# Attention with hand-placed projection steps: projection units of a batch on other steps, norming in place on ScalarE

## What is computed

```python
h = group_norm(x, w, b)                       # 32 groups of 16 channels
q, k, v = split(einsum('oc,bcn->bon', qkv_w, h) + qkv_b)   # 8 heads of 64
attn = softmax(einsum('bhdi,bhdj->bhij', q, k) * 64 ** -0.5)
out = einsum('bhij,bhdj->bhdi', attn, v)
x1 = x + einsum('oc,bcn->bon', proj_w, out) + proj_b
```

## Time and profile before

| what | us |
|---|---|
| median of three runs | 3378.47 |
| the profiled execution | 3384.99 |
| its span, first to last instruction | 3383.0 |
| PE busy | 2937.5 (87%) |
| DVE busy | 2124.9 (63%) |
| ACT busy | 1588.4 (47%) |
| POOL busy | 443.2 (13%) |

### The profile page before, as it was taken

One profiled execution on the slowest core, in us unless ns is written; L12 is line 12 of the kernel. 1 busy time (PEld: TensorE's weight loads), 2 busy tenths in 40 slices (PEclk: granted clock), 3 DMA queues, 4 the chain that ended last, 5 costly groups with the idle time before them and its releaser, 6 DMA issues. The chain is left out here.

```text
span 3383.0 us, 34913 instructions
## 1 busy us (share of the span) xinstructions
PE 2937.5 (87%) x12368; PEld 2375.9 (70%) x12368; DVE 2124.9 (63%) x3224; ACT 1588.4 (47%) x1935; POOL 443.2 (13%) x193
## 2 busy tenths in 40 slices
PE   4998998999899999989998998999755877777877
PEld 2776886788688778868876786888544666656656
DVE  5686767768776776777677677757624435435443
ACT  2565656556564555656456555646521222212221
POOL 1012111100210120021012002011101100111000
PEclk8999999999899999989999999999977988888888
DMA  6222131222123122212312131232030100111100
GB/s 217 60 57 63 54 110 44 63 88 76 57 59 113 48 63 71 84 37 79 113 47 70 53 100 38 82 102 58 19 121 25 50 37 37 37 37 50 43 31 25
DMA packets 131084, 221.52 MB, mean 65 GB/s; under 512 B 50048, under 2 KB 50304, under 8 KB 130432
## 3 DMA queue, kind: packets, MB, share of 16 engines
q1 hardware_dynamic: 130944, 219.69, 21.1%
HBM read 143.34 MB, written 42.21 MB: 55 GB/s over the span
## 5 line engine op out<-in xcount | busy, mean ns | idle before, releaser
L590 DVE TENSOR_REDUCE row_max<-pmax 128x1 f32<-128x512 f32 x1024 | 703.2, 687 | 602.5 <-PE pmax L389 599.0
L484 ACT ACTIVATE p_high<-ring 128x1024 fp32r<-128x1024 f32 x512 | 525.1, 1026 | 730.6 <-PE ring L410 730.4
L606 DVE TENSOR_TENSOR p_low<-p_full,p_high 128x1024 fp32r<-128x1024 f32 x512 | 665.1, 1299 | 6.3 <-ACT p_full L487 6.3
L389 PE MATMUL pmax<-k_high_low,q_high_high 128*128 128x512 f32 x1024 | 459.5, 449 | 98.9 <-DVE row_max L590 96.1
L487 ACT ACTIVATE p_full<-ring 128x1024 f32<-128x1024 f32 x512 | 520.9, 1017 | 0.0
L389 PEld LDWEIGHTS pmax<-k_high_low,q_high_high 128*128 128x128 f32 x1024 | 316.5, 309 | 221.0 <-DVE row_max L590 135.5
L767 POOL TENSOR_TENSOR o_normed<-num_den,o_normed 64x1024 f32<-64x1024 f32 x64 | 173.1, 2705 | 1961.4 <-DMA o_normed<-rec_rows 1943.6
L426 PE MATMUL pv<-p_high,v_high 128*128 128x512 f32 x1024 | 411.9, 402 | 0.0
L427 PE MATMUL pv<-p_high,v_low 128*128 128x512 f32 x1024 | 406.9, 397 | 0.0
L344 PE MATMUL fill<-h_high,w_high 128*128 128x512 f32 x768 | 309.2, 403 | 39.4 <-DVE q_low_max L619 17.1
L410 PE MATMUL ring<-q_low_max,k_high_one 65*128 65x512 f32 x1024 | 330.9, 405 | 1.9 <-DMA q_low_max<-row_max_top 1.9
(11 more groups left out here) (161 smaller groups left out, 3748.6 us busy)
## 6 DMA issues: line engine op xcount, KB each, us to landing
x_tiles<-in_x SPq DMA_DIRECT2D x64, 512.0 KB, 5.4
w_high<-w_split SPq DMA_DIRECT2D x128, 256.0 KB, 2.9
w_low<-w_split SPq DMA_DIRECT2D x128, 256.0 KB, 2.9
k_high_one<-k_high_low SPq DMA_DIRECT2D x128, 128.0 KB, 2.3
q_high_high<-q_high_high SPq DMA_DIRECT2D x128, 128.0 KB, 2.3
o_normed<-rec_rows SPq DMA_DIRECT2D x64, 256.0 KB, 3.5
...
```

What stands on the lines that cost most here:

```text
L389: mm(pmax[:, :], q1[:, q_slot(h), first:first + HALF - 3:4], k1[:, k_slot(h), n * HALF:(n + 1) * HALF], start=True, stop=True).then_inc(s_ ...
L484: nc.scalar.activation(ph[:, r, :], ring[:, r, :], ACT.Exp, scale=ATT_SCALE).then_inc(s_ph, 1)
L590: nc.vector.reduce_max(mcol[:, h % 2, n, i:i + 1], pmax[:, :], AX_X).then_inc(s_mx, 1)
L606: tt(pl[:, r, :], p32[:, r, :], ph[:, r, :].bitcast(F32), ALU.subtract).then_inc(s_pl, 1)
```

## The change

The units of each pair get their steps from a table, and several functions change engine or place.

- **Projection units.** The steps of the units of one batch, before and after (a and b are the two halves of a spread unit, "+" joins units of one step; o is numbered in its order, two for each of four tiles):

| head | before: step: unit | after: step: unit |
|---|---|---|
| 0 | 0,1: k0; 2,3: k1; 4,5: q0; 6,7: none | 0: k0; 1: k1; 2: v0; 3: v1a+vt0; 4: v1b; 5: vt1; 6,7: q0 |
| 1 | 0: q1; 1: v0; 2: v1+vt0; 3: o1; 4: o2+vt1; 5,6,7: o3 to o5 | 0: q1; 1 to 7: o1 to o7 |
| 2 | 0,1,2: o6 to o8; 3,4: k0; 5,6: k1; 7: q0 | 0: o8; 1,2: k0; 3,4: k1; 5,6: q0; 7: none |
| 3 | 0,1: q1; 2,3: v0; 4: v1a; 5: v1b+vt0; 6: none; 7: vt1 | 0,1: q1; 2,3: v0; 4: v1a+vt0; 5: v1b; 6: vt1; 7: none |
| 4 | 0,1: k0; 2,3: k1; 4,5: q0; 6: g0; 7: none | 0,1: k0; 2: g0; 3,4: k1; 5: g1; 6,7: q0 |
| 5 | 0: q1+g1; 1: v0; 2: v1+vt0; 3: none; 4: vt1; 5,6,7: none | 0,1: q1; 2,3: v0; 4: v1a+vt0; 5: v1b; 6: vt1; 7: none |
| 6 | 0,1: none; 2,3: k0; 4,5: k1; 6,7: q0 | the same |
| 7 | 0,1: q1; 2,3: v0; 4: v1a; 5: v1b+vt0; 6: none; 7: vt1 | 0,1: q1; 2,3: v0; 4: v1a+vt0; 5: v1b; 6: vt1; 7: none |

- **Group norm.** The statistics move to steps 3.1, 3.3, 3.4 and 3.5, the scale to 5.0.
- **Norming.** ACT writes the full normed value in place in steps 5.1 to 5.4 (`normed_full`), and reads it again for the high part in 5.5, 5.6, 5.7 and 6.0 (`normed_high`). The norming on DVE is gone. `h_low` stays on POOL, at the same place in its order, and waits for the high part. In the prologue ACT does both for each tile.
- **SP.** The store of the last tile of x1, the load after it and the reload of x each move one step up.

```diff
+PAIR_STEPS = (begins(0, 1, 6, 8, 2, 3, 3, 5, whole=(("k", 0), ("k", 1), ("v", 0), ("q", 1))),
...
-            for s in range(5):
-                put(b, 3 + s, o[s])
-            for s in range(3):
-                put(a + 2, s, o[5 + s])
+            for s in range(7):
+                put(b, 1 + s, o[s])
+            put(a + 2, 0, o[7])
...
-            put(a, 6, ("g", b0 + 1, 0))
-            put(b, 0, ("g", b0 + 1, 1))
+            put(a, 2, ("g", b0 + 1, 0))
+            put(a, 5, ("g", b0 + 1, 1))
...
-            def normed(b, t):
-                if t == 0:
-                    act.wait_ge(s_gab, b + 1)
-                    if b > 0:
-                        act.wait_ge(s_unit, unit(("v", PAIRS * b - 1, 1)))
+            def normed_full(b, t):
+                act.wait_ge(s_gab, b + 1)
                 a, c = gs[:, 6, t:t + 1], gs[:, 7, t:t + 1]
-                nc.scalar.activation(hh[:, t, :], xs[:, t, :], ACT.Identity, bias=c, scale=a).then_inc(s_hh, 1)
+                nc.scalar.activation(xs[:, t, :], xs[:, t, :], ACT.Identity, bias=c, scale=a).then_inc(s_h32, 1)
+            def normed_high(b, t):
+                if b > 0 and t >= 1:
+                    act.wait_ge(s_unit, unit(("v", PAIRS * b - 1, 1)))
+                act.wait_ge(s_h32, bt((b, t)))
+                nc.scalar.activation(hh[:, t, :], xs[:, t, :], ACT.Copy).then_inc(s_hh, 1)
...
-                if h % HEADS == 5 and b < BATCH and 3 <= s <= 6:
-                    normed(b, s - 3)
+                if h % HEADS == 5 and b < BATCH and 1 <= s <= 4:
+                    normed_full(b, s - 1)
+                if h % HEADS == 5 and b < BATCH and s >= 5:
+                    normed_high(b, s - 5)
+                if h % HEADS == 6 and b < BATCH and s == 0:
+                    normed_high(b, CT - 1)
...
-            def normed_full(b, t):
-                dve.wait_ge(s_hh, bt((b, t)))
-                dve.wait_ge(s_gab, b + 1)
-                nc.vector.tensor_scalar(xs[:, t, :], xs[:, t, :], gs[:, 6, t:t + 1], gs[:, 7, t:t + 1],
-                                        ALU.mult, ALU.add).then_inc(s_h32, 1)
...
-                    if h % HEADS == 4 and 1 <= s <= 4:
-                        tile_stats(b, s - 1)
-                    if h % HEADS == 5 and s == 2:
+                    if h % HEADS == 3 and s in (1, 3, 4, 5):
+                        tile_stats(b, (1, 3, 4, 5).index(s))
+                    if h % HEADS == 5 and s == 0:
                         group_scale(b)
-                    if h % HEADS == 5 and 3 <= s <= 6:
-                        normed_full(b, s - 3)
...
+            def rstd(b):
+                pool.wait_ge(s_gst, gst((b, "var")))
+                if b > 0:
+                    pool.wait_ge(s_on, HEADS * (b - 1) + 4)
...
             def h_low(b, t):
-                pool.wait_ge(s_h32, bt((b, t)))
+                pool.wait_ge(s_hh, bt((b, t)))
```

More of the change, by code:

```diff
@@ L106, with begins @@
 HALF_UNITS = (0, 1)
+def begins(k0, k1, q0, q1, v0, v1, vt0, vt1, whole=()):
+    begin = {("k", 0): k0, ("k", 1): k1, ("q", 0): q0, ("q", 1): q1, ("v", 0): v0, ("v", 1): v1}
+    return {**{u: (s, u in whole) for u, s in begin.items()}, ("vt", 0): vt0, ("vt", 1): vt1}
+PAIR_STEPS = (begins(0, 1, 6, 8, 2, 3, 3, 5, whole=(("k", 0), ("k", 1), ("v", 0), ("q", 1))),
+              begins(1, 3, 5, 8, 10, 12, 12, 14),
+              begins(0, 3, 6, 8, 10, 12, 12, 14),
+              begins(2, 4, 6, 8, 10, 12, 12, 14))
 def parts_by_step():
@@ L125, in parts_by_step @@
             o = [("o", b0 - 1, t, i) for t in range(CT) for i in range(2)]
-            for s in range(5):
-                put(b, 3 + s, o[s])
-            for s in range(3):
-                put(a + 2, s, o[5 + s])
+            for s in range(7):
+                put(b, 1 + s, o[s])
+            put(a + 2, 0, o[7])
         if n == ALL_PAIRS:
             continue
-        first = {0: 0, 1: 3, 2: 0, 3: 2}[kind]
-        if kind == 1:
-            spread(a, 3, ("k", n, 0))
-            spread(a, 5, ("k", n, 1))
-            put(a, 7, ("q", n, 0))
-        else:
-            spread(a, first, ("k", n, 0))
-            spread(a, first + 2, ("k", n, 1))
-            spread(a, first + 4, ("q", n, 0))
-        if kind in (0, 2):
-            put(b, 0, ("q", n, 1))
-            put(b, 1, ("v", n, 0))
-            put(b, 2, ("v", n, 1))
-            put(b, 2, ("vt", n, 0))
-            put(b, 4, ("vt", n, 1))
-        else:
-            spread(b, 0, ("q", n, 1))
-            spread(b, 2, ("v", n, 0))
-            spread(b, 4, ("v", n, 1))
-            put(b, 5, ("vt", n, 0))
-            put(b, 7, ("vt", n, 1))
+        begin = PAIR_STEPS[kind]
+        for name, i in (("k", 0), ("k", 1), ("q", 0), ("q", 1), ("v", 0), ("v", 1)):
+            at_step, whole = begin[name, i]
+            (put if whole else spread)(a + at_step // STEPS, at_step % STEPS, (name, n, i))
+        for i in range(2):
+            at_step = begin["vt", i]
+            put(a + at_step // STEPS, at_step % STEPS, ("vt", n, i))
         if kind == 2 and b0 + 1 < BATCH:
-            put(a, 6, ("g", b0 + 1, 0))
-            put(b, 0, ("g", b0 + 1, 1))
+            put(a, 2, ("g", b0 + 1, 0))
+            put(a, 5, ("g", b0 + 1, 1))
     return at
@@ L734, in _ @@
             group_scale(0)
-            for t in range(CT):
-                normed_full(0, t)
             for w in range(6, 16):
@@ L773, in o_low @@
                                         ALU.subtract).then_inc(s_ol, 1)
-            def rstd(b):
-                pool.wait_ge(s_gst, gst((b, "var")))
-                nc.gpsimd.tensor_tensor(gs[:, 5, :], gs[:, 4, :], gs[:, 0, :], ALU.pow).then_inc(s_rstd, 1)
-            def h_low(b, t):
-                pool.wait_ge(s_h32, bt((b, t)))
-                nc.gpsimd.tensor_tensor(hl[:, t, :], xs[:, t, :], hh[:, t, :].bitcast(F32),
-                                        ALU.subtract).then_inc(s_hl, 1)
             pool.wait_ge(s_dset, 1)
@@ L912, in step @@
                         after_store(u[1], u[2] - 1)
+                if h >= HEADS and h % HEADS == 2 and s == 2:
+                    store(h // HEADS - 1, CT - 1)
                 if h >= HEADS and h % HEADS == 2 and s == 3:
-                    store(h // HEADS - 1, CT - 1)
-                if h >= HEADS and h % HEADS == 2 and s == 4:
                     after_store(h // HEADS - 1, CT - 1)
-                if h % HEADS == 6 and s == 3 and h // HEADS + 1 < BATCH:
+                if h % HEADS == 6 and s == 2 and h // HEADS + 1 < BATCH:
                     for t in range(CT):
```

9 lines of the change are left out of this document (7 added, 2 removed).

## The result

The changed kernel takes 3286.39 us, the median of four runs (3283.82 to 3294.43), against 3378.38 for the kernel before on the same chip (four runs, 3375.32 to 3380.99). The ratio is 0.9732, its 95% interval 0.9713 to 0.9751, so 92 us are gained. The forecast was 3289.

A forecast was written before the change was run, and what follows sets the result against it. PE was taken as the bound, losing time only where idle or paced by DVE and POOL. Regrouping 1.05 us plus stalls from 26.35 to 14.45 gave 12.95 a batch, 89.8 in all: 3289, 8-in-10 range 3240 to 3341.

The forecast's parts named there:

- forecast case: Whole kernel: stalls fall from 26.35 to 14.45 us a batch, giving 3289; chance 0.64, own range 3255 to 3330.
- Units two places ahead: Heads 1 and 5: waits for units completed just a step before vanish; the 1.9 us in head 1 and 5.1's stall go.
- The scale in 5.0: Steps 5.0 and 5.1: DVE waits 1.3 us for rstd behind o_low; 1.4 plus 0.6 for slower clock, 2.0 in all.
- normalise beside p_low: Steps 0.6 and 7.5, likewise 5.5: POOL's normalise starts first and delays DVE's p_low, leaving 0.85 us each.
- Heads 2 and 3: Stalls of 1.2 us in head 2 around empty step 2.7, and 1.3 in head 3 around 3.5.
- The chain from 5.5: Steps 5.5 to 6.1: each h_low delays a p_low and stretches the next step; 7.5 us, weighted 6.65 with clock.
- ACT at nothing: Head 5: ACT's added norming, 4.1 us a batch, is covered and costs nothing; without cover 1 us.
- Outside the six batches: Batch 0 gains 11.05 us, batch 7's old and new stalls cancel, the prologue gains 1.
- mild blocks: Rival: p_low goes first each time and POOL fits behind; stalls about 8.5 us, 3250 or less, say 3243; chance 0.12.
- Spread blocks: Rival: h_low meets a p_low every step and the clock falls; six to nine us more a batch, 3340 to 3352; 0.13.
- Only-shifted stalls: Rival: new wait in 5.0 and 5.1 costs about 5 us, units wait in head 0 or 2; 3372 to 3385; 0.06.
- The slower rival: Every two-input operation from 5.5 to 6.1 loses 2.6 to 3.7 us; stalls 29.8 a batch, 3395; chance 0.05.

The follow-up runs named there:

- e2: Kernel before the change, its units, statistics and scale kept, but ACT alone norms, both operations in one step, 5.3 to 5.6: 3342.09 us, ratio 0.9886.
- e6: Changed kernel with POOL holding normalise behind the p_low of step 5 of the next head and each h_low behind its step's p_low: 3243.06 us.
- e9: Changed kernel with only normalise held on POOL until the p_low of step 5 of the next head is done, h_low not held: 3235.34 us.
- e11: The changed kernel itself, unaltered, timed once more on another chip run: 3291.95 us, ratio 0.9739.
- e3: Changed kernel with h_low computed for only 64 of 1024 columns from the second batch on, the rest left as they were: 3257.07 us, ratio 0.9625.

## Why the prediction was right

It gave 3289 with 0.64 for the forecast case, and that case is what the trace shows. By head, in us, mean of batches 1 to 6:

| heads | priced | predicted | measured |
|---|---|---|---|
| 0 | 36.95 | 37.8 | 37.0 |
| 1 | 44.0 | 44.0 | 44.05 |
| 2 | 33.5 | 34.7 | 35.0 |
| 3 | 31.85 | 33.15 | 35.1 |
| 4 | 31.1 | 32.7 | 32.85 |
| 5 and 6 | 62.95 | 71.6 | 70.5 |
| 7 | 31.85 | 32.7 | 32.5 |
| sum | 272.2 | 286.65 | 287.0 |

The stalls are 14.8 a batch where 14.45 was foretold. The terms one by one:

- **Units two places ahead.** Right. Head 1 is at its price and 5.1 no longer waits for a unit. e2, with the old table, has both stalls (2.17 in 1.5, 3.71 in 5.1).
- **The scale in 5.0.** Right in place and cause, 1.25 against 1.3 for DVE's wait. The 0.6 for a slower clock did not come: 5.0 and 5.1 together cost 1.40, not 2.0. PE idled only 0.93 in a row there.
- **normalise beside p_low.** Right as a mechanism. In 0.6 it left 0.15, not 0.85. In 7.5 to 7.7 it left 0.68 (0.55, −0.18 and 0.31), where 0.85 was foretold.
- **Heads 2 and 3.** Undersized. 2.7 and 3.0 cost 2.07, not 1.2: the empty step loses in its successor as much again. 2.4 costs 0.43 that I had not seen: in 2.3, in the third batch, DVE idles 1.09 at the reciprocals until their DMA lands. In 3.5 to 3.7 the stall is 2.26, not 1.3: in the third batch p_low took 3.44, and v_low and the statistics stood behind it. In e6 and e9, with normalise behind p_low and the same DVE work, these three steps have 0.22. The changed kernel's timeline there, POOL and DVE:

```profile
781.01 2.39 POOL L764 TENSOR_TENSOR o_normed<-num_den,o_normed 64x1024 f32<-64x1024 f32 x1 [20.01 <-DMA o_normed<-rec_rows]
781.04 3.44 DVE L613 TENSOR_TENSOR p_low<-p_full,p_high 128x1024 fp32r<-128x1024 f32 x1
...
785.01 0.68 DVE L635 TENSOR_TENSOR v_low<-fill,v_high 128x512 fp32r<-128x512 f32 x1
785.61 1.27 DVE L686 BATCH_NORM_STATS2 bn_parts<-x_tiles 128x6 f32<-128x512 f32 x2
```

  Normalise starts 0.03 ahead and is done at 783.40, yet p_low ends only at 784.48, 1.08 later, for its own 1.22. With the 1.03 in 3.0 it makes head 3 longer than foretold by 2 us. The terms of heads 2 and 3, 2.5 in all, measured 4.7.
- **The chain from 5.5.** Right in its mechanism. By hand it was 0.85, 1.35, 2.1, 1.1 and 2.1 for 5.5 to 6.1, 7.5 in all. Measured means are 0.80, 1.38, 2.10, 1.29 and 0.60. The first four fit within 0.2. The last came only in two of the six batches. In the other four the fourth h_low starts behind the p_low, by 0.52 in the third batch (868.91 against 868.39), and takes the delay itself. The clock was 0.76 over 14.1 us where the earlier trace rows had 0.52. What it cost is not separated from the measured means, which hold it. The sum was 6.65 against 6.17, but 6.65 is a weighted term, seven tenths of 7.5 and three tenths of 2.05, with 0.75 for the clock. For a batch with the chain the prediction had 7.5 + 0.75 = 8.25, and all six of these batches had it, at 6.17. So a chain sized 2 us too large was met by a weight below one. The chance of 7 in 10 for the chain came out as 6 of 7 batches in one execution and 5 of 7 in another (e11).
- **ACT at nothing.** Right. e3 keeps all of ACT's work, and its steps 5.6 to 6.1 are 0.2 over their price together. ACT's lines in the changed kernel, both within 0.04 us of what I used:

```profile
L526 ACT ACTIVATE x_tiles<-x_tiles,gn_small 128x1024 f32<-128x1024 f32 x32 | 39.6, 1239 | 1.3 <-DVE gn_small L667 1.3
L534 ACT ACTIVATE h_high<-x_tiles 128x1024 fp32r<-128x1024 f32 x32 | 34.0, 1064 | 0.1
```

- **Outside the six batches.** Batch 0 gained 13.9, not 11.05, as it drew the mild case. Batch 7 gained 4.4, where I let its stalls cancel. The prologue gained 0.1, not 1. Batches 1 to 6 gained 80.3, not 77.7, since the third batch before was 0.75 below the mean of its six.

In all the span shrank by 98.7 where 89.8 was foretold. The forecast still came within 3 us, as I subtracted 6.5 for the distance of the profiled execution from its median, and the changed kernel's profiled execution lies on its median. So two errors of opposite sign met, and inside the batch those of heads 0, 5 and 6 (2.0 too much) met those of heads 2 and 3 (2.2 too little), and the chain by itself was met by its weight. The mechanism was foretold; that the total was hit so closely was in good part luck.

One line of my tests was wrong in itself: "head 5 takes about 41" put all 6.65 of the chain into head 5, though 6.0 and 6.1 belong to head 6. By the terms it is about 38, and 37.5 was measured. Two bounds are slightly off by their own terms: the low ends give 3235, not 3233, and the 8.5 us of stalls of the mild rival give 3247, not 3243.

The rivals: mild blocks (chance 0.12) is the state of single batches, and of all of them once POOL is held back (e9). Spread blocks did not come: in the third batch the clock stayed at 1.00 in all heads but 5 and 6, where it was 0.95, and in four batches of six the fourth h_low left its p_low alone. The second batch, at 29.6, came nearest, with 8.6 of stalls from 5.5 to 6.2. Only-shifted stalls fell with the missing unit waits. The slower rival needed losses of 2.6 to 3.7 for each operation. In the profile of the changed kernel row_max_top takes 2.04 at most and p_low there 3.33, which is 2.1 over its 1.22.
